# Causal attention with feed-forward on one core: the diagonal mask of the transposed scores moves from TensorE to VectorE

## What is computed

```python
scores = jnp.einsum('bhqd,bhkd->bhqk', q, k) * scale
causal = jnp.tril(jnp.ones((S, S), dtype=bool))
scores = jnp.where(causal, scores, jnp.finfo(scores.dtype).min)
probs = jax.nn.softmax(scores, axis=-1)
attn = jnp.einsum('bhqk,bhkd->bhqd', probs, v)
```

## Time and profile before

| | |
|---|---|
| median of three runs | 1855.29 us |
| the profiled execution | 1856.94 us |
| its span, first to last instruction | 1855.1 us |
| granted TensorE clock, mean share of 2.4 GHz | 0.995 |
| TensorE, VectorE, ScalarE, GpSimd busy | 98%, 60%, 38%, 37% of the span |

### The profile page before, as it was taken

The page is one execution under the profiler, slowest core; times in us unless marked ns, Lnnn a source line. Parts: engine busy times, 40 slices in busy tenths (PEclk is TensorE's granted clock), DMA queues, the critical chain, the costliest instruction groups (busy, mean ns, idle before and its releaser), DMA issues.

```text
span 1855.1 us, 29601 instructions
## 1 busy us (share of the span) xinstructions
PE 1812.8 (98%) x10880; PEld 1373.3 (74%) x10880; DVE 1116.3 (60%) x1708; ACT 699.5 (38%) x1151; POOL 692.7 (37%) x672
## 2 busy tenths in 40 slices
PE   7989999999999999899999999999999999999998
PEld 6867666666666664368888888888888888888887
DVE  5416666666666564547766665675666567566644
ACT  3313555656566565013322232232233233223222
POOL 1431558678677677012221222222222222222221
PEclk9999999999999999999999999999999999999999
DMA  8775043242342300621011101101110110110002
GB/s 280 219 215 149 9 89 69 53 89 61 60 90 51 70 8 13 215 69 34 12 23 34 34 0 34 34 0 34 34 32 2 34 34 0 34 34 0 0 0 91
DMA packets 73107, 108.64 MB, mean 59 GB/s; under 512 B 24704, under 2 KB 44784, under 8 KB 69360
## 3 DMA queue, kind: packets, MB, share of 16 engines
q1 hardware_dynamic: 73008, 107.34, 21.2%
HBM read 74.04 MB, written 29.59 MB: 56 GB/s over the span
## 4 chain that ended last, share of the span: by engine, by line
PE 59%; DVE 0%; issue 0%
PE p_gate L51 6%; PE p_up L51 6%; PE p_gate L49 6%; PE p_gate L50 6%; PE p_up L49 6%; PE p_up L50 6%; PE p_out L51 6%; PE p_out L50 6%; PE p_out L49 6%; PE p_out L1298 1%; PE p_gate L1298 1%; PE p_up L1298 1%; DVE acc L1228 0%
## 5 line engine op out<-in xcount | busy, mean ns | idle before, releaser
L1140 POOL TENSOR_SCALAR poly<-poly 128x1024 f32<-128x1024 f32 (+1 forms) x65 | 71.5, 1100 | 837.5 <-ACT poly L1102 837.5
L589 POOL TENSOR_TENSOR e_sum<-e_sb 128x512 f32<-128x512 f32 (+2 forms) x320 | 331.4, 1064 | 106.7 <-PE p_o L856 103.2
L720 DVE TENSOR_REDUCE max_part<-p_s 128x1 f32<-128x512 f32 x384 | 240.6, 682 | 57.2 <-PE p_s L791 56.7
L657 ACT ACTIVATE e_sb<-p_v 128x512 f32<-128x512 f32 (+3 forms) x427 | 216.4, 552 | 142.1 <-PE p_v L818 76.5
L1203 DVE SCALAR_TENSOR_TENSOR inter<-inter,gate 128x1024 f32<-128x1024 f32 (+1 forms) x65 | 78.6, 1209 | 248.3 <-ACT inter L1108 247.5
L791 PE MATMUL p_s<-k_stack,q_stack 96*128 96x512 f32 (+3 forms) x640 | 217.1, 393 | 3.0 <-DMA k_stack<-qk_scratch 2.4
L716 DVE CUSTOM_DVE_ANT_0 recip<-p_s,score_mask 128x128 bf16<-128x128 f32 (+3 forms) x256 | 119.6, 486 | 166.6 <-PE p_s L791 164.4
L49 PE MATMUL p_gate<-xn_hi,w_hi 128*128 128x512 f32 x512 | 199.8, 390 | 0.0
L1101 ACT ACTIVATE gate<-p_gate 128x1024 f32<-128x1024 f32 (+1 forms) x65 | 65.9, 1015 | 354.5 <-PE p_gate L51 354.5
L51 PE MATMUL p_gate<-xn_hi,w_lo 128*128 128x512 f32 x512 | 199.4, 389 | 0.0
L50 PE MATMUL p_gate<-xn_lo,w_hi 128*128 128x512 f32 x512 | 199.3, 389 | 0.0
(11 more groups left out here) (143 smaller groups left out, 3067.8 us busy)
## 6 DMA issues: line engine op xcount, KB each, us to landing
q_stack<-qk_scratch SPq DMA_DIRECT2D x48, 256.0 KB, 7.1
k_stack<-qk_scratch SPq DMA_DIRECT2D x48, 256.0 KB, 8.0
qk_scratch<-out_hi SPq DMA_DIRECT2D x32, 256.0 KB, 2.6
qk_scratch<-out_lo SPq DMA_DIRECT2D x32, 256.0 KB, 3.3
scales<-in_gate_up_s SPq DMA_DIRECT2D x128, 64.0 KB, 2.3
xn_lo_scratch<-xn_lo SPq DMA_DIRECT2D x4, 1024.0 KB, 5.2
v_scratch<-o_sb SPq DMA_DIRECT2D x16, 256.0 KB, 2.5
xn_lo<-xn_lo_scratch SPq DMA_DIRECT2D x1, 4096.0 KB, 16.9
```

The costliest lines, as they stand in the source:

```text
L589: nc.gpsimd.tensor_tensor(e_sum[:, n % SUM_BUFS, 0:w], e_sb[:, x % E_BUFS, skip:skip + w], e_sb[:, y % E_BUFS, 0:w], ALU.add).then_inc(poo ...
L657: nc.scalar.activation(e_sb[:, x % E_BUFS, 0:w], bank_st(x)[:, 0:w], ACT.Exp, scale=SCALE).then_inc(exp_done, 1)
L720: nc.vector.reduce_max(part, p_s[:, slot[n] % S_BUFS, 0:w], AX.X).then_inc(maxed, 1)
```

## The change

On the diagonal the transposed scores' matmul now closes its accumulation and raises `st_ready` itself, as elsewhere. The mask matmuls are gone. VectorE waits for `st_ready`, adds `mask_k` (bf16, in SBUF) to the first 128 columns of the bank in place, and raises a new semaphore `st_masked`; the exponentials of these pieces wait for that. VectorE's queue takes the adds in the order of TensorE's issue: two adds, then the maxima of the units that TensorE computes behind those two pieces, and so on, by the same table (`BESIDE`). In the opening steps two adds come behind each two maxima.

```diff
+    BESIDE = {0: (0, 1, 2), 2: (3,), 4: (4, 5), 6: (6,)}
+    DIAG_PIECES = {x: n for n, x in enumerate(x for x in range(NSTEP * PIECES) if DIAG[x // PIECES % NS])}
...
+        st_masked = sem("st_masked")
...
-                act.wait_ge(st_ready, x + 1)
+                if x in DIAG_PIECES:
+                    act.wait_ge(st_masked, DIAG_PIECES[x] + 1)
+                else:
+                    act.wait_ge(st_ready, x + 1)
...
+            def mask_t(x):
+                if x in DIAG_PIECES:
+                    dve.wait_ge(st_ready, x + 1)
+                    here = bank_st(x)[:, 0:P]
+                    nc.vector.tensor_tensor(here, here, mask_k[:, :], ALU.add).then_inc(st_masked, 1)
+
             for n in range(FIRST):
                 unit_max(n)
...
+                if n >= FIRST_V and (n - FIRST_V) % 2:
+                    mask_t(n - FIRST_V - 1)
+                    mask_t(n - FIRST_V)
...
+                if x in DIAG_PIECES:
+                    for n in BESIDE:
+                        mask_t(x + n)
+                        mask_t(x + n + 1)
+                        for part in BESIDE[n]:
+                            some_units(part, 8)
+                    some_units(7, 8)
+                else:
+                    some_units(0, 1)
...
-                                        stop=not DIAG[s])
-                if not DIAG[s]:
-                    last.then_inc(st_ready, 1)
-
-            def mask_t(x):
-
-                if piece(x)[0] < NSTEP:
-                    nc.tensor.matmul(bank_st(x)[:, 0:P], ident[:, :], mask_k[:, :], start=False,
-                                     stop=True).then_inc(st_ready, 1)
+                                        stop=True)
+                last.then_inc(st_ready, 1)
...
-                mask_t(x)
-                mask_t(x + 1)
...
-                        mask_t(x + n)
-                        mask_t(x + n + 1)
-                        for part in {0: (0, 1, 2), 2: (3,), 4: (4, 5), 6: (6,)}[n]:
+                        for part in BESIDE[n]:
                             some_units(part, 8)
```

More of the change, by code:

```diff
@@ L764, in _, with some_units @@
                 units = units_of(k)
[L765 to L769, removed]
+                x = (GS * k + LEAD) * PIECES
+                def some_units(part, parts):
+                    for n in units[part * len(units) // parts:(part + 1) * len(units) // parts]:
+                        unit_max(n)
+                        for p_, r in BATCHES[k]:
+                            if n + 1 == p_ * NU + UNITS_TO[r]:
+                                join_parts(p_, r)
+                if x in DIAG_PIECES:
[7 more added lines that the diff above has]
+                    some_units(0, 1)
                 if p == PAIRS - 1 and s in (20, 24, 28):
```

## The result

| | before | after |
|---|---|---|
| median | 1856.01 us (4 runs, 1853.86 to 1856.95) | 1927.12 us (4 runs, 1923.05 to 1928.79) |
| the profiled execution | 1856.94 us, span 1855.1 | 1925.80 us, span 1924.0 |
| granted TensorE clock, mean | 0.995 | 0.972 |

The ratio is 1.0382 (95% interval 1.0361 to 1.0402): 71 us slower, where 49 were forecast, and 3 us beyond the end of the range. The direction is right, and so is the chain over m2, E2 and S5. Two things in the forecast are not: the number of times that TensorE's clock falls, and the sentence that VectorE has room in total.

A forecast was written before the change was run, and what follows sets the result against it. TensorE, busy 98% of the span, was taken as the bound, waiting in attention for exponentials. Queue 38.7 us plus clock 10 gave +49 on the profiled 1856.94, so 1904 us as median; range 1885 to 1924.

The forecast's parts named there:

- m2, E2 and S5: Diagonal groups: piece 2's add, late behind three maxima, delays its exponential, then piece 5's scores, by 1.2 to 1.7 us.
- VectorE has room in total: VectorE over the whole span: it can take 73 us more work; only the order of its queue costs.
- masks removed: TensorE, diagonal pieces: 128 pairs of mask matmuls at 0.10 us each save 12.8 us, if TensorE never waits.
- one add; in a row: VectorE: a mask add costs 0.285 us, 0.21 in a row of adds; bounds 0.18 and 0.42.
- queue term: Diagonal groups: products start later because exponentials wait for VectorE's adds, masks' saving included; 38.7 us together.
- kinds 1, 4, 8, 9: Diagonal groups by k mod 10: row sums and products start 1.05, 1.37, 1.17 and 1.5 us later.
- price of a fall: TensorE in attention: each stretch at 1.2 GHz instead of 2.4 GHz costs about 1.7 us.
- number of falls: TensorE's clock drops to 1.2 GHz in some of 31 diagonal groups: 6 taken by judgement, from 0 to 14.
- clock term: TensorE in diagonal groups: 6 drops to half clock at 1.7 us each add 10 us.
- The opening: The opening four rounds of two units and two pieces: VectorE's adds make them 1.4 us longer.
- D4: VectorE's maximum 4, whose bank TensorE's second turn of the maxima needs: no later, with 0.1 to 0.3 us of room.
- rival 2: Heavier: adds near 0.42 us, late second turns, or clock falls in half the groups; 1913 to 1940 us, chance 0.14.

The follow-up runs named there:

- experiment 4: The kernel before, with no mask on the transposed scores on either engine and row maxima taken without their mask: 1845.51 us, ratio 0.9941.
- experiment 1: The changed kernel, with TensorE repeating score matmuls in its two longest stalls of a diagonal group, same result: 1886.60 us, ratio 1.0164.
- Experiment 3: The kernel before, masks still on TensorE, with 256 further VectorE maxima over SBUF at the adds' places that nothing waits for: 1882.31 us, ratio 1.0131.
- experiment 2: The changed kernel with VectorE's order altered in diagonal groups, the adds of pieces 0, 1, 2 ahead of the first maximum: 1894.05 us, ratio 1.0202.
- experiment 5: The changed kernel with adds early and TensorE's turns of the maxima moved behind the second step's products: 1882.76 us, ratio 1.0127.

## Why the prediction was right and wrong

| step of the prediction | forecast | measured |
|---|---|---|
| masks removed | -12.8 us | -11.8 (experiment 4) |
| one add; in a row | 0.285; 0.21 us | 0.291; 0.20 |
| m2, E2, S5 in k = 29 | 3.30, 3.63, 4.17 | 3.22, 3.54, 4.08 |
| queue term, kinds 1, 4, 8, 9 | 1.05, 1.37, 1.17, 1.5 | 0.97, 1.21, 0.97, 1.13 (experiment 1) |
| queue term, all | 38.7 us | 30 (ratio of experiment 1) |
| price of a fall | 1.7 us | 1.6 |
| number of falls | 6 (0 to 14) | 27 |
| clock term | 10 us | 40 |

**Removal, add, chain.** These held, S5 to 0.09 us. (By the prediction's own terms 38.7 + 10 is 48.7, so its 1905.8 is 0.2 high, which changes nothing.) The add's price is that of the nearest row. The queue's rate settles the one rule that was weighed: two adds of 0.29 us take 0.49 together, so the next one doesn't wait for the whole record of the one before it, and the 7 us on top that the prediction took from one reading of the Trainium skill (VectorE: DVE Perf Modes, The DRAIN you can't avoid) did not come.

**Queue term.** 9 us too high. Each group came out 0.1 to 0.4 us shorter than laid out, kind 9 most; that is 5.8 us of it. In k = 29 of experiment 1, S5 is 0.09 early, and from there to the row sums it is 1.50 us (401.65 to 403.15) for the 1.66 of my timetable: what follows S5 is closer together than I had it. The opening, put at +1.4, is +0.7. Group 74, put at +0.3, is 0.44 shorter than before: without units there TensorE keeps what the removed masks give back.

**"VectorE has room in total; it is the order that costs."** This failed, though it did not change the sum. Experiment 3, in which nobody waits for the added work, is 20 us longer in its diagonal groups; experiment 2, with the chain over m2 taken apart, 25. I had written that D4 is 0.1 to 0.3 us short of the second turn, which is to say that load costs almost as much as order, and then used it only against rival 2. Experiment 4 shows the same from the other side: in kind 9, TensorE 0.5 us earlier only waits for D3 and D4.

**The number of falls.** This is the step that failed and that carries the error: the clock term, 6 falls for 10 us where 27 were found, for 40. The price of one was right, the six were "judgement". The rows that I had said more: the earlier trace rows show a fall where TensorE had been busy for 3.25 of 4.09 us with 24 matmuls. My own timetable for group 29 had eight matmuls start in nearly four microseconds, a far emptier stretch than that one. Had the row been taken at its word, each of the 29 groups would have been a candidate: 29 x 1.7 = 49 us instead of 10. With the measured 27 and the measured price the same sum gives 30 + 27 x 1.6 = 73, against 71 measured. Without the queue term's 9 us too many the forecast would have missed by more: in part the two errors cancelled. It was the clause in rival 2, "falls in half the groups", that came true, and more than that: 22 of the 31. Rival 2 had a chance of 0.14. The Trainium skill bears on this (TensorE: Matmul & The Clock Gate, A second HAM failure mode: psum-queue depth-cycling). It tells of a kernel whose TensorE idles briefly between groups of matmuls as it cycles through PSUM banks, often enough that its clock goes back and forth between the two levels. The trace agrees: no wait of TensorE's in k = 29 is longer than 1.21 us, and it fell.

Which groups fall is not settled. Kind 1 is, with kind 8, the one with the smallest queue term and falls every time; groups 18 and 28 do the same work and only one falls. Something of where a group's idle time lies, or when, decides it, and no run here was made for that.

## What to carry to other kernels

When a change puts idle time into a TensorE that was just short of free-running, price the clock first, group by group: here each microsecond of the queue term brought 1.3 more at the lower clock (40 us for 30), and filling the waits with repeats of a matmul told the two terms apart in one run. An engine's free share over the whole span says nothing of a stage; before giving it work, ask in each group what last waits for it (here the second turn for D4), and look at the load by itself with idle instructions that nobody waits for.

## What the runs showed that I had not expected

- 195 repeated matmuls, whose results are only written again, made the changed kernel 40 us faster (1927.1 to 1886.6); 100 of them in the kernel of experiment 5 brought nothing clear of noise (1882.8 to 1878.0).
- Whether a group falls can alternate between groups of the same content: k = 18 at 1.00 and 8.52 us, k = 28 at 0.83 and 10.13 us.
- Moving the turns of the row maxima by 16 products is free in the kernel before (ratio 1.0002), and worth 10 us and more of queue term in one that is late.
- GpSimd's select on a 128x128 tile of SBUF takes 0.26 us in a row of four, VectorE's add in PSUM 0.20 in a row; it was the select's place in GpSimd's queue that cost.
